# Local attention layers: the value matrix as the loaded operand on two column halves, the row sums divided after the turn, and the output projection between the two turned halves

## What is computed

```
h = shift_token(x)
q, k, v = split(h @ wqkv, 3)                 # 8 heads of 64, f32
q = l2norm(q) * qs;  k = l2norm(k) * ksc
q, k = rotary_xpos(q, k)
# windows of 128 tokens; each looks at itself and the window before (256 keys)
sim = einsum('bhwid,bhwjd->bhwij', bq, bk)   # masked
attn = softmax(sim)
out = einsum('bhwij,bhwjd->bhwid', attn, bv)
x = x + out @ wo
# then a dense part: shift_token, layer norm, w1, a * gelu(g), w2, residual
```

## Time and profile before

| | |
|---|---|
| median of 3 runs | 5213.57 us (5209.88 to 5215.06) |
| profiled execution | 5215.38 us, its span 5213.7 us |
| TensorE busy, share of the span | 95% |
| VectorE | 79% |
| ScalarE | 59% |
| GpSimd | 20% |
| mean granted TensorE clock | 0.979 |

### The profile page before, as it was taken

How to read it: one execution, slowest core, us unless ns; L and a number is a source line. 1 busy time by engine, 2 the same in 40 slices (tenths; PEclk the granted TensorE clock), 3 DMA queues, 4 the chain that set the end, 5 groups by cost and what they waited for, 6 DMA issues and landing times. The chain is left out here.

```text
span 5213.7 us, 115536 instructions
## 1 busy us (share of the span) xinstructions
PE 4972.5 (95%) x33636; PEld 2623.9 (50%) x33636; DVE 4142.1 (79%) x8806; ACT 3087.1 (59%) x4572; POOL 1047.5 (20%) x828
## 2 busy tenths in 40 slices
PE   6799999999999999999999999997999898999899
PEld 3333333333333333333333333334888776888766
DVE  7588888888888888888888888894777644777655
ACT  4366666666666666666666666665665422566521
POOL 3311111111111111111211111103333201333211
PEclk9699999999999999999999999998999899999999
DMA  6312212212122122121221211223000000000010
GB/s 200 80 51 56 57 51 57 56 51 57 51 57 57 51 57 57 50 57 50 57 57 51 56 51 51 53 53 134 1 0 0 18 0 18 1 0 0 4 42 20
DMA packets 255913, 243.96 MB, mean 47 GB/s; under 512 B 86412, under 2 KB 199248, under 8 KB 253904
## 3 DMA queue, kind: packets, MB, share of 16 engines
q1 hardware_dynamic: 244592, 214.83, 15.6%
q0 software_dynamic: 8976, 26.77, 2.5%
q10 hardware_dynamic: 2256, 1.21, 0.1%
HBM read 210.72 MB, written 31.72 MB: 47 GB/s over the span
## 5 line engine op out<-in xcount | busy, mean ns | idle before, releaser
L840 DVE TENSOR_REDUCE group_max<-shared_ps 128x1 f32<-128x512 f32 x4048 | 2674.4, 687 | 387.5 <-PE shared_ps L588 315.3
L755 ACT ACTIVATE probs<-scores 128x1024 f32<-128x1024 f32 x2048 | 1986.9, 1022 | 986.0 <-DVE scores L815 707.7
L588 PE MATMUL shared_ps<-keys,max_queries 96*128 96x512 bf16 x4052 | 1406.4, 382 | 2.1 <-DVE group_max L840 1.0
L615 PE MATMUL scores<-queries,keys 98*128 98x512 bf16 (+3 forms) x4096 | 1224.7, 370 | 4.6 <-ACT probs L755 2.9
L630 PE MATMUL out_ps<-probs,values 128*17 128x512 f32 x8192 | 1078.9, 598 | 5.4 <-ACT probs L755 0.6
L588 PEld LDWEIGHTS shared_ps<-keys,max_queries 96*128 96x128 bf16 x4052 | 388.9, 96 | 1095.9 <-DVE group_max L840 599.4
L309 POOL TENSOR_TENSOR near_window<-near_bias,one_f 128x1536 bf16<-128x1536 f32 x128 | 351.6, 2747 | 2736.9 <-DVE max_parts L834 2128.4
L615 PEld LDWEIGHTS scores<-queries,keys 98*128 98x128 bf16 x4096 | 366.1, 98 | 304.9 <-ACT probs L755 60.7
L1342 POOL TENSOR_TENSOR norm<-norm,layer_expo 128x16 f32<-128x16 f32 x64 | 186.3, 2911 | 696.3 <-DVE norm L1727 696.3
L1601 ACT ACTIVATE sim_prob<-sim_prob,shift,norm 128x256 f32<-128x256 f32 x512 | 299.6, 590 | 10.0 <-DVE shift L1797 10.0
L641 PEld LDWEIGHTS shared_ps<-block_q,block_table 96*128 96x128 bf16 x4096 | 235.7, 114 | 106.3 <-issue 66.3
(11 more groups left out here) (205 smaller groups left out, 5713.8 us busy)
## 6 DMA issues: line engine op xcount, KB each, us to landing
keys<-k_parts SPq DMA_DIRECT2D x384, 96.0 KB, 2.1
values<-v_wide SPq DMA_DIRECT2D x448, 68.0 KB, 1.9
keys<-k_parts SPq DMA_DIRECT2D x384, 64.0 KB, 2.0
keys<-k_parts SPq DMA_DIRECT2D x128, 132.0 KB, 2.4
head_q<-q_parts POOLq DMA_DIRECT2D x96, 128.0 KB, 5.4
keys<-k_parts SPq DMA_DIRECT2D x384, 32.0 KB, 1.8
queries<-q_parts SPq DMA_DIRECT2D x768, 16.0 KB, 1.7
max_queries<-q_parts SPq DMA_DIRECT2D x762, 16.0 KB, 1.6
```

The lines of the kernel that those rows point to most:

```text
L588: mm = pe.matmul(bank, max_queries[par][:, t * P:(t + 1) * P], keys[par][0:ROWS, (t + TPC * g) * P:(t + TPC * (g + 1)) * P], start=True, s ...
L615: mm = pe.matmul(out[:, 0:cut], keys[par][:, tile * P:(tile + 1) * P], queries[par][:, 0:cut], start=True, stop=True)
L755: act.activation(probs[s % 4][:], scores[s % 2][:], ACT.Exp).then_inc(exp_done, 1)
L840: dve.tensor_reduce(group_max[par][:, k:k + 1], bank, AX.X, ALU.max).then_inc(max_read, 1)
```

## The change

The values become the loaded (stationary) operand of the weighing: each product loads 64 columns of v and streams the 128 columns of a turned probability block, and writes the output already turned, even heads to PSUM partitions 0 to 63, odd heads to 64 to 127. The output needs no turn of its own any more. The division by the sums then acts on the turned output, for which the reciprocal sums are widened to 512 columns on ScalarE (`spread_inv`), turned on TensorE (`turn_total`, at the head of the next window, into `o_ps`) and copied by ScalarE (`keep_total`). VectorE divides with one multiplication that writes `o_T` itself. `project_o` is put between the two halves of `turn_prob`. Beside that, VectorE makes the rotation table first in the window and rotates q before the norm's sums, ScalarE puts the first exponential between the two squares, GpSimd adds q before it takes the power, and the semaphore `first_in` is dropped for a count on `fixed_in`.

```diff
@@ -1191,7 +1191,8 @@
             prob_T = win("prob_T", [P, 2 * LHEADS, P])
-            o_tok = win("o_tok", [P, LHEADS, LD])
+            total_T = win("total_T", [P, KI, P])
+            inv_wide = win("inv_wide", [P, LHEADS, LD])
             o_T = win("o_T", [P, KI, P])
@@ -1338,13 +1339,13 @@
             def rotate(g, par):
+                pool.wait_ge(S.turned_b, g * 2 + 2)
+                pool.tensor_tensor(rot_a[:, 0:LHEADS, :], rot_a[:, 0:LHEADS, :], rot_b[:, 0:LHEADS, :], ALU.add
+                                   ).then_inc(S.rot_sum, 1)
                 pool.wait_ge(S.norm_guard, g + 2)
                 pool.tensor_tensor(norm[par][:], norm[par][:],
                                    expo[:, 0:2 * LHEADS].rearrange("p (h a) -> p h a", a=1),
                                    ALU.pow).then_inc(S.norm_ready, 1)
-                pool.wait_ge(S.turned_b, g * 2 + 2)
-                pool.tensor_tensor(rot_a[:, 0:LHEADS, :], rot_a[:, 0:LHEADS, :], rot_b[:, 0:LHEADS, :], ALU.add
-                                   ).then_inc(S.rot_sum, 1)
@@ -1427,8 +1428,8 @@
-            def turn_prob(g):
-                for h in range(LHEADS):
+            def turn_prob(g, half):
+                for h in range(half * 4, half * 4 + 4):
                     if h % 4 == 0:
@@ -1438,27 +1439,31 @@
+            def turn_total(g):
+
+                pe.wait_ge(S.inv_spread, g + 1)
+                pe.wait_ge(S.win_done, g + 1)
+                for i in range(KI):
+                    mm = pe.transpose(o_ps[:, i * P:(i + 1) * P],
+                                      inv_wide[:, 2 * i:2 * i + 2, :].rearrange("p h d -> p (h d)"), ident_f[:])
+                mm.then_inc(S.total_turned, 1)
+
             def weigh(g, at):
                 pe.wait_ge(S.prob_T_act, g + 2)
                 pe.wait_ge(S.prob_T_dve, g + 2)
-                pe.wait_ge(S.win_done, g + 1)
-                for h in range(LHEADS):
+                pe.wait_ge(S.total_kept, g + 1)
+                for i in range(KI):
                     for c, v in enumerate((v_kept[at - 1], v_kept[at])):
-                        j = slot(h)
-                        mm = pe.matmul(o_ps[:, j * LD:(j + 1) * LD], prob_T[:, 2 * j + c, :],
-                                       v[:, h * LD:(h + 1) * LD], start=c == 0, stop=c == 1)
+                        for odd in range(2):
+                            h = 2 * i + odd
+                            mm = pe.matmul(o_ps[odd * LD:(odd + 1) * LD, i * P:(i + 1) * P],
+                                           v[:, h * LD:(h + 1) * LD], prob_T[:, 2 * slot(h) + c, :],
+                                           start=c == 0, stop=c == 1)
                 mm.then_inc(S.pv_ready, 1)
-            def turn_o(g):
+            def project_o(g):
                 pe.wait_ge(S.o_ready, g + 2)
-                for i in range(KI):
-                    mm = pe.transpose(o_ps[:, i * P:(i + 1) * P],
-                                      o_tok[:].rearrange("p h d -> p (h d)")[:, i * P:(i + 1) * P], ident_f[:])
-                mm.then_inc(S.o_T_ready, 1)
-
-            def project_o(g):
-                pe.wait_ge(S.o_T_kept, g + 1)
                 for i in range(KI):
@@ -1469,21 +1474,22 @@
                     turn_tile(g + 1, 1 - par)
+                if before:
+                    turn_total(g - 1)
                 similarities(g, par)
                 if more:
                     project(g + 1, 1 - par)
                 if before:
                     weigh(g - 1, (at - 1) % RING)
-                turn_prob(g)
+                turn_prob(g, 0)
                 if before:
-                    turn_o(g - 1)
+                    project_o(g - 1)
+                turn_prob(g, 1)
                 if more:
                     turn_qk(g + 1)
-                if before:
-                    project_o(g - 1)
-                if not more:
+                else:
+                    turn_total(g)
                     weigh(g, at)
-                    turn_o(g)
                     project_o(g)
...
+            def square(g, j):
+                if j == 0:
+                    act.wait_ge(S.norm_guard, g + 1)
...
@@ -1592,20 +1598,27 @@
-            def exps(g, par):
-                act.wait_ge(S.shift_ready, g + 1)
-                act.wait_ge(S.prob_T_ready, g * 2 + 1)
-                act.wait_ge(S.total_inv, g + 1)
-                for h in range(LHEADS):
+            def exps(g, par, heads):
+                if heads[0] == 0:
+                    act.wait_ge(S.shift_ready, g + 1)
+                    act.wait_ge(S.prob_T_ready, g * 2 + 1)
+                    act.wait_ge(S.total_inv, g + 1)
+                for h in heads:
                     head = slot(h)
                     ins = act.activation(prob[:, h, :], sim[:, h, :], ACT.Exp, bias=shift[:, head:head + 1],
                                          scale=norm[par][:, head, :], accum_out=total[:, h, :])
                     if h % 4 == 3:
                         ins.then_inc(S.exp_done, 1)
-            def keep_o(g):
-                act.wait_ge(S.o_T_ready, g + 1)
-                act.activation(o_T[:].rearrange("p i n -> p (i n)"), o_ps[:], ACT.Copy).then_inc(S.o_T_kept, 1)
+            def spread_inv(g):
+                act.wait_ge(S.total_inv, g + 2)
+                act.activation(inv_wide[:], inv_total[:].to_broadcast([P, LHEADS, LD]), ACT.Copy
+                               ).then_inc(S.inv_spread, 1)
+
+            def keep_total(g):
+                act.wait_ge(S.total_turned, g + 1)
+                act.wait_ge(S.o_ready, g + 1)
+                act.activation(total_T[:].rearrange("p i n -> p (i n)"), o_ps[:], ACT.Copy).then_inc(S.total_kept, 1)
@@ -1619,8 +1632,14 @@
                     keep_hT(g + 1, 1 - par)
-                    square(g + 1)
-                exps(g, par)
+                if before:
+                    keep_total(g - 1)
+                if more:
+                    square(g + 1, 0)
+                exps(g, par, range(1))
+                if more:
+                    square(g + 1, 1)
+                exps(g, par, range(1, LHEADS))
                 if isinstance(w, int) and w == LAYER - 3:
@@ -1628,12 +1647,11 @@
                                ACT.Copy).then_inc(S.prob_T_act, 1)
-                if before:
-                    keep_o(g - 1)
+                spread_inv(g)
                 if more:
                     keep_qk(g + 1, 1 - par)
                 else:
-                    keep_o(g)
+                    keep_total(g)
@@ -1743,15 +1762,8 @@
                 dve.wait_ge(S.pv_ready, g + 1)
-                dve.wait_ge(S.total_inv, g + 2)
-                for half in range(2):
-                    heads = slice(4 * half, 4 * half + 4)
-                    ins = dve.tensor_tensor(o_tok[:, heads, :].rearrange("p (a b) d -> p b a d", b=2),
-                                            o_ps[:, half * 4 * LD:(half + 1) * 4 * LD]
-                                            .rearrange("p (b a d) -> p b a d", b=2, d=LD),
-                                            inv_total[:, heads, :].rearrange("p (b a) d -> p b a d", b=2)
-                                            .to_broadcast([P, 2, 2, LD]), ALU.mult)
-                ins.then_inc(S.o_ready, 1)
+                dve.tensor_tensor(o_T[:].rearrange("p i n -> p (i n)"), o_ps[:],
+                                  total_T[:].rearrange("p i n -> p (i n)"), ALU.mult).then_inc(S.o_ready, 1)
@@ -1783,6 +1795,7 @@
                 if more:
+                    scale_table(w + 1, g + 1)
                     keep_low(g + 1, 1 - par)
@@ -1797,17 +1810,17 @@
                 if more:
-                    scale_table(w + 1, g + 1)
+                    scale_rotate(g + 1, 0)
                     sum_squares(g + 1, 1 - par)
-                    scale_rotate(g + 1)
+                    scale_rotate(g + 1, 1)
                 if before:
                     divide_o(g - 1)
                 if more:
                     add_k(g + 1)
                     divide_norm(g + 1, 1 - par)
                 dve.wait_ge(S.exp_done, g * 2 + 3)
-                dve.wait_ge(S.o_ready, g + 1)
-                dve.reciprocal(inv_total[:], total[:]).then_inc(S.total_inv, 1)
+                dve.reciprocal(inv_total[:].rearrange("p (a b c) d -> p a b (c d)", b=2, c=2),
+                               total[:].rearrange("p (a c b) d -> p a b (c d)", b=2, c=2)).then_inc(S.total_inv, 1)
                 dve.wait_ge(S.prob_T_ready, g * 2 + 3)
...
+            def scale_rotate(g, j):
...
```

More of the change, by code:

```diff
@@ L1575, in keep_hT @@
                 act.activation(hT_b[0][par][:, 1:P + 1], v_ps[:, P:2 * P], ACT.Copy).then_inc(S.hT_kept, 1)
-            def square(g):
-                act.wait_ge(S.norm_guard, g + 1)
-                for j in range(2):
-                    act.wait_ge(S.qkv_ready, g * 3 + j + 1)
-                    act.activation(squares[:, j * LHEADS:(j + 1) * LHEADS, :],
```

(43 more changed lines are left out.)

10 lines of the change are left out of this document (5 added, 5 removed).

## The result

The changed kernel takes 5086.03 us in the median of 4 runs (5084.27 to 5092.16) against 5213.02 us of the kernel before in 4 runs beside it: a ratio of 0.9759, 95% interval 0.9742 to 0.9776. The forecast was 5100. Its profiled execution took 5092.2 us with a span of 5090.4, which is 123 us less than that of before, where the sum had said 113.

What follows compares the result with a forecast made beforehand. A window was bound by 15.1 us of TensorE work plus 0.85 waiting for VectorE's chain. Saving 51.3 (windows), 4.1 (end) and 1.3 (window 0), 56.7 a layer, 113.4 in all, gave 5102 from 5215.4, stated as 5100; range 5070 to 5145.

Steps and rivals of the forecast that it cites:

- The weighing: TensorE's weighing per window: from 3.52 to 2.08 us, 1.75 for 16 side-by-side pairs plus 0.33 for array switching.
- wait for `rot_a`: TensorE's q/k transposes: the 0.85 us wait for VectorE's rotation result goes, as it is ready near 9.1, needed at 9.9.
- the wait before the sum turn: TensorE, head of the next window: a new wait of about 0.6 us, released by `add_o`.
- The second chain: Window path through q/k transposes ending at 10.86, ScalarE's two copies and similarities: 14.14 us, just under the longest chain.
- The window: Steady window: chain from projection through weighing, division, output projection, `add_o`, sum turn and similarities sums to 14.24 us.
- C: Weighing: the column halves don't overlap, weighing 3.75, window 15.9, time 5205 us; chance 0.04.
- D: Weighing: every change of half is paid as a switch, weighing 8.4, window 20.5, time 5490 us; chance 0.04.
- B: VectorE becomes the bound, its reduce slowed by GpSimd's addition: window 14.6, 5121 us, or 5140 with semaphore steps; chance 0.27.
- A: Array switching costs nothing visible: weighing 1.75, window 14.0, time 5086 us; range down to window 13.8 (5075); chance 0.15.
- The serial end of a layer: After the last window of each layer, through the last projection: 4.1 us less.
- From the first projection to window 1: Window 0 of each layer: the wait for GpSimd's addition goes, 1.3 us less.
- The term of the windows: Windows 1 to 31: 30 windows at 1.71 us less each, 51.3 us a layer.

Runs made afterwards that it cites:

- early_add: Changed kernel with VectorE's addition of the projected output ahead of its copy of the turned probabilities: 5076.95 us, ratio 0.9741 to the kernel before.
- four_blocks: Changed kernel with the sum turn's four transposes spread between the head pairs of the similarities: 5166.35 us, ratio 0.9909 to the kernel before.
- the second trace of before: Kernel before, unaltered, run and traced again: 5211.41 us.
- the second of the change: Changed kernel, unaltered, run and traced again: 5090.47 us.
- old_order: Changed kernel with the orders of VectorE, ScalarE and GpSimd as before the change: 5168.02 us, ratio 0.992 to the kernel before.
- halves_alone: Changed kernel with old engine orders and output projection behind the q/k transposes: 5265.78 us, ratio 1.0106 to the kernel before.

## Why the prediction was right

*The weighing.* Forecast 2.08 with its switches, of which 1.75 for 16 pairs. The block is 1.90, the projection ahead of it is 4.38 long where it was 4.28, and the first eight transposes behind it 0.93 where half of 1.75 is 0.88: 2.05 in all. The reading that carried this, four strips that run together in the earlier trace rows, held for two halves as well; the experiment with one half at a time takes the gain back.

*The waits.* The wait for `rot_a` went, the wait before the sum turn came with 0.65 (forecast "about 0.6"), `add_o` is its releaser, and early_add shows that the cause is the place in the queue. The second chain, forecast at 14.14 (its terms add up to 14.12), was measured once the first was gone: 14.05.

*The window.* 14.24 forecast, 14.30 measured. Its small terms: division to projection 0.68 and 0.1 to be seen for 0.75; projection 1.77 for 1.73; sum turn 0.56 for 0.53.

*The rivals.* C and D are refuted by the single starts of the weighing in the changed kernel: pairs are 0.109 apart and the two halves of a pair start 0.006 or 0.007 apart. B's mechanism (the reduce slowed by GpSimd's addition) didn't come, it stays at 1.22. A's low end didn't come either: a way into and out of a split array costs 0.37 by four_blocks.

*What was mis-sized.* The time came out 14 us lower than forecast. Two terms were too small. The serial end of a layer, forecast 4.1 less, is 5.0 less (39.4 and 39.3 in the second trace of before, 34.4 and 34.3 in the second of the change). From the first projection to window 1 I had forecast 1.3 less for each layer. The norm is waited for twice there, in the layer's first rotation and in window 0, and I had counted GpSimd's 1.28 once. The first rotation gives 1.4 (from the start of v's projection to the q/k transposes: 7.82 to 7.86 before, 6.43 to 6.50 after, over both traces). Window 0 gives 1.3 at full clock (from the start of v's projection to the similarities of window 1: 10.11 in the first trace of before, 8.78 in the second of the change). That is 2.7 in all. These two terms are 1.8 + 2.8 = 4.6 us too small over both layers.

The term of the windows was not too small. In the second traces they gain 52.5 a layer for 51.3 forecast, but of that 1.7 and 1.9 are one step of the kernel before: its window 1 took 17.71 and 17.90 us for 15.97, with a granted clock of 0.76 and 0.74 in its first 8 us. In the first trace of before, layer one's window 1 had a clock of 1.00 and took 15.98, and the gain there is 50.8. The low clock also made before's way into window 1 longer in the second trace (33.3 and 34.1 us for 32.8 and 32.6 in the first), where its q/k transposes took 1.97 us for 1.09. Window 1 was longer in three of the four layers traced of the kernel before, and in none of the four of the change. With the old orders it also started below full clock (0.93 and 0.94 in old_order, 0.94 and 0.95 in halves_alone), with the new orders alone at 1.00 twice. So the orders may earn up to 2 us a layer by the clock, a term that the forecast did not have; that the order is the cause is not shown. So of the 14 us, 4.6 are the two small terms, 5.6 are low clock in the second trace of before (3.7 in window 1, 1.9 on the way to it), and the windows give 1.2 less than forecast. Some 5 I can't place; the runs of one kernel lie 5 us (before) and 8 us (after) apart.

*What the experiments add.* The parts do not add up. From the kernel before, the reorderings alone give 55 us, the halves alone cost 57, and together with the placement they give 127. TensorE's own work fell by 1.5 us a window (15.10 with the reorderings alone, 13.61 where nothing waits any more), and that is worth nothing as long as the chain through VectorE and GpSimd, or the projection at the end, sets the window.

## What to carry to other kernels

Count a saving on the busiest engine only after walking the whole cycle of waits with the new length in it; then look at what stands in the queue in front of the instruction that the new wait is for, since moving one addition ahead of one copy was worth 9 us here (13 by windows 1 to 31) and splitting one semaphore another 31 (25 by the windows). Where f32 products stream only 64 columns for 128 loaded, try them the other way round, on two halves of the array, in alternating order and in one block: here 32 instructions fell from 3.52 to 1.90 us, alternating was worth 1.36 of that, and each further way into and out of a split array cost 0.37.

## What I had not expected of the hardware

- With the products of one half all ahead of the other's, six instructions near the seam still started 0.006 to 0.058 us behind the last one: the block was 3.26 us where one by one would be 3.5.
- VectorE's addition of two SBUF operands took 0.68, 1.26 or 1.72 us for the same shape, according to how long GpSimd's addition (1.28) had yet to run when it started. The division by the norm did the same beside GpSimd's copy of a tile (0.69 alone, 0.98 and 1.00).
- TensorE's granted clock in the same 20 us of the same kernel was 0.51 and 0.50 in one execution and 0.83 and 0.96 in another, 6.9 us apart. One profiled pair of executions can mislead by that much at a layer's serial end.
